# Counting a repeated class of edges: two pairs more per set beside the experts, one set per chunk after them, one set of buffers

## The reference, cut to what matters

```python
h = (x_flat @ W_gat).reshape(M, HEADS, NUM_EXPERTS)
e = leaky_relu(a_src[src] + a_dst[dst], 0.2)      # per edge and head
ee = exp(e - segment_max(e, dst)[dst])
denom = segment_sum(ee, dst)
agg = segment_sum(h[src] * (ee / denom[dst])[:, :, None], dst)
scores = layernorm(agg).mean(heads)
...
for ei in range(4):                               # four experts, every token
    hh = gelu(x @ W1[ei] + b1[ei])
    out += gate[:, ei] * (hh @ W2[ei] + b2[ei])
```

## Time and profile before

| | |
|---|---|
| median of 3 runs | 3698.13 us (3690.57 to 3706.22) |
| the profiled execution's own time | 3702.64 us |
| span of its profile | 3701.0 us |
| mean granted TensorE clock | 0.907 of full speed |
| leading chunks, about 1740 to 2243 us of the span | 503 us |
| late chunks, about 2243 to 2355 us | 112 us |

### The profile page before, as it was taken

How to read it: one execution, slowest core, us unless ns; L and a number is a source line. 1 busy time by engine, 2 the same in 40 slices (tenths; PEclk the granted TensorE clock), 3 DMA queues, 4 the chain that set the end, 5 groups by cost and what they waited for, 6 DMA issues and landing times. The chain is left out here.

```text
span 3701.0 us, 55128 instructions
## 1 busy us (share of the span) xinstructions
PE 2732.4 (74%) x16350; PEld 1679.7 (45%) x16350; DVE 2369.3 (64%) x4532; ACT 1369.6 (37%) x2278; POOL 1087.6 (29%) x1035
## 2 busy tenths in 40 slices
PE   0442123999999999955888785246999999949994
PEld 0332122444444444424665564244655555526662
DVE  9999797787888878776444446794444444433333
ACT  5310100777777878753344341033000000012221
POOL 0000103777773000001655565000111111114442
PEclk9999999999999999975898895557999999969997
DMA  5999895554545445431111111342333333324446
GB/s 194 355 368 410 321 396 192 182 198 176 187 175 196 186 174 201 158 100 29 43 45 42 42 42 16 104 161 81 104 104 103 108 108 103 108 70 124 126 122 195
DMA packets 233854, 568.88 MB, mean 154 GB/s; under 512 B 52113, under 2 KB 93944, under 8 KB 225134
## 3 DMA queue, kind: packets, MB, share of 16 engines
q1 hardware_dynamic: 146006, 376.34, 29.7%
q10 hardware_dynamic: 56152, 163.80, 11.8%
q0 software_dynamic: 31552, 27.13, 3.3%
HBM read 443.12 MB, written 125.87 MB: 154 GB/s over the span
## 5 line engine op out<-in xcount | busy, mean ns | idle before, releaser
L1881 PE MATMUL at_out<-at_pt,top_H 128*128 128x512 f32 x2048 | 931.7, 601 | 34.8 <-ACT at_agg L1733 29.8
L1723 ACT ACTIVATE at_rl<-at_qrow,at_less,at_steep 128x512 f32<-128x512 f32 x1024 | 741.5, 804 | 89.6 <-DVE at_pt L1809 49.6
L1809 DVE SCALAR_TENSOR_TENSOR at_pt<-at_rl,at_turned 128x1024 f32<-128x1024 f32 x512 | 626.2, 1223 | 157.2 <-PE at_out L1881 80.7
L2098 PE MATMUL at_out<-at_parts,at_a 128*128 128x387 bf16 x4096 | 689.3, 328 | 28.8 <-DVE at_parts L2171 15.7
L1881 PEld LDWEIGHTS at_out<-at_pt,top_H 128*128 128x128 f32 x2048 | 373.0, 190 | 439.2 <-issue 396.6
L2098 PEld LDWEIGHTS at_out<-at_parts,at_a 128*128 128x128 fp8e4 x4096 | 399.4, 98 | 305.6 <-issue 36.8
L903 POOL DMA_INDIRECT rec<-at_part x304 | 384.2, 1264 | 104.9 <-issue 93.2
L1161 POOL DMA_INDIRECT edges_GT<-tab,gat_RC x320 | 339.9, 1062 | 237.0 <-DMA edges_GT<-tab,gat_RC 153.0
L2046 POOL DMA_INDIRECT slots<-at_Y,at_dest x128 | 123.2, 962 | 650.7 <-DVEq L2276 614.6
L648 PE MATMUL pack_bp<-top_weights,sort_recs 128*128 128x8 bf16 x1696 | 76.0, 170 | 233.4 <-DMA sort_recs<-in_adj_dram 233.4
L2549 PE MATMUL ex_hp<-ex_XS,ex_WB 128*128 128x512 f32 (+1 forms) x472 | 217.7, 598 | 1.9 <-DMA ex_WB<-wts 1.9
(11 more groups left out here) (551 smaller groups left out, 3695.4 us busy)
## 6 DMA issues: line engine op xcount, KB each, us to landing
sort_recs<-in_adj_dram SPq DMA_DIRECT2D x212, 512.0 KB, 8.9
at_adj<-in_adj_dram SPq DMA_DIRECT2D x192, 512.0 KB
adjT<-at_turned ACTq DMA_DIRECT2D x64, 1024.0 KB
at_a<-adjT SPq DMA_DIRECT2D x128, 512.0 KB
bucket_raw<-in_adj_dram ACTq DMA_DIRECT2D x120, 512.0 KB, 10.2
ex_WB<-wts SPq DMA_DIRECT2D x42, 533.0 KB
y<-f_YB ACTq DMA_DIRECT2D x64, 256.0 KB
f_YB<-y SPq DMA_DIRECT2D x16, 1024.0 KB, 10.4
```

The source lines that it names most:

```text
L1723: ins = nc.scalar.activation(RL[v % NBUF][:, k, :], qrow[:], ACT.Relu, bias=less[:], scale=steep[:, u:u + 1])
L1809: nc.vector.scalar_tensor_tensor(out=PT[v % NBUF][:], in0=RL[v % NBUF][:], scalar=1.0, in1=AT[v // VP % 2][:, 2 * (v % VP):2 * (v % VP) + ...
L1881: ins = nc.tensor.matmul(OUT[:], H[:, u, :], PT[v % NBUF][:, k, :], start=(u == 0), stop=(u == T - 1))
L2098: ins = nc.tensor.matmul(OUT[:, g, x, 0:3 * D1], ones[c % NBUF][:, j, x * P:(x + 1) * P], parts[:, u].rearrange("p k d -> p (k d)"), start ...
```

## The change

Early sets grow from 4 to 6 pairs (3 groups of two pairs), the three late sets of 4 pairs in a late chunk become one set of 4, and there is one set of buffers for all. The pairs counted in this stage go from 17 x 4 + 12 x 4 = 116 to 17 x 6 + 4 x 4 = 118, and `HELD` from 464 to 472. The waits for `late_used` ahead of a late set go.

```diff
-EARLY_SETS, LATE_SETS = 17, 12
-HELD = (EARLY_SETS + LATE_SETS) * 2 * GC
+EARLY_SETS, LATE_SETS = 17, 4
+EARLY_GROUPS, LATE_GROUPS = 3, 2
+HELD = (EARLY_SETS * EARLY_GROUPS + LATE_SETS * LATE_GROUPS) * GC
...
-    PAIRS = 4
+    PAIRS = 2 * EARLY_GROUPS
...
-            OPC = [[spare[1 + s][...] for n in range(PAIRS)] for s in range(2)]
+            OPC = [spare[1 + n // 4][...] for n in range(PAIRS)]
...
-                    def count_hots(s, at, done):
-                        for n in range(PAIRS):
+                    def count_hots(pairs, at, done):
+                        for n in range(pairs):
...
+                    def early_hots(j):
+                        count_hots(2 * EARLY_GROUPS, j * (EARLY_GROUPS * GC), same_hot)
+
+                    def late_hots(i):
+                        count_hots(2 * LATE_GROUPS, (EARLY_SETS * EARLY_GROUPS + i * LATE_GROUPS) * GC, late_hot)
...
-                    def late_hots(g, r):
-                        for i in range(g * IN_LATE, (g + 1) * IN_LATE):
-                            dve.wait_ge(late_used, (off + r) * LATE_SETS + i + 1)
-                            dve.sem_inc(passed, 1)
-                            count_hots((1 + i) % 2, EARLY_SETS + i, late_hot)
...
-                            add_counts(late_used, (off + r) * LATE_SETS + (g + 1) * IN_LATE + 2)
+                            add_counts(late_used, (off + r) * LATE_SETS + g + 1)
...
                     def late_counts(g, r, k):
                         pe.wait_ge(lk_read, k + 2)
                         pe.sem_inc(passed, 1)
-                        for i in range(g * IN_LATE, (g + 1) * IN_LATE):
-                            pe.wait_ge(late_hot, (off + r) * LATE_SETS + i + 1)
-                            pe.sem_inc(passed, 1)
-                            count((1 + i) % 2, range(PAIRS), i % IN_LATE == 0, (i + 1) % IN_LATE == 0).then_inc(late_used, 1)
+                        pe.wait_ge(late_hot, (off + r) * LATE_SETS + g + 1)
+                        pe.sem_inc(passed, 1)
+                        count(range(2 * LATE_GROUPS), 2 * LATE_GROUPS - 1).then_inc(late_used, 1)
...
                                     if e == 2:
                                         early_ready(l * EARLY_SETS + q, k)
-                                        count(g % 2, range(PAIRS // 2), True, False)
+                                        count(range(PAIRS // 2), PAIRS - 1)
                                     output(u + e - 1, e - 1)
                                     if e == 2:
-                                        count(g % 2, range(PAIRS // 2, PAIRS), False, True).then_inc(same_used, 1)
+                                        count(range(PAIRS // 2, PAIRS), PAIRS - 1).then_inc(same_used, 1)
...
                         early_ready(l * EARLY_SETS + EARLY_SETS - 1, (off + LEAD) * RG - 1)
-                        count((EARLY_SETS - 1) % 2, range(PAIRS), True, True).then_inc(same_used, 1)
+                        count(range(PAIRS), PAIRS - 1).then_inc(same_used, 1)
```

More of the change, by code:

```diff
@@ L965, in edge_gates @@
     LEAD = NG // RG
-    PAIRS = 4
-    IN_LATE = LATE_SETS // RG
+    PAIRS = 2 * EARLY_GROUPS
     HK = CK // 2
@@ L971, in edge_gates @@
     assert HID == K * P and K == 2 and NE == 4 and RG == 4 and LEAD == 4
-    assert EARLY_SETS == LEAD * RG + 1 and LATE_SETS == RG * IN_LATE
+    assert EARLY_SETS == LEAD * RG + 1 and LATE_SETS == RG and LATE_GROUPS <= EARLY_GROUPS
     with Phase(nc, "gat") as ph:
@@ L1061, in edge_gates @@
             value = spare[0][:, 4 * HELD:4 * HELD + P * GC].rearrange("p (v c) -> p v c", c=GC)
-            OPC = [[spare[1 + s][:, n * P * GC:(n + 1) * P * GC].rearrange("p (v c) -> p v c", c=GC) for n in range(PAIRS)] for s in range(2)]
-            OFC = [[spare[3][:, (s * PAIRS + n) * T * GC:(s * PAIRS + n + 1) * T * GC].rearrange("p (v c) -> p v c", c=GC)
-                    for n in range(PAIRS)] for s in range(2)]
+            OPC = [spare[1 + n // 4][:, n % 4 * P * GC:(n % 4 + 1) * P * GC].rearrange("p (v c) -> p v c", c=GC) for n in range(PAIRS)]
+            OFC = [spare[3][:, n * T * GC:(n + 1) * T * GC].rearrange("p (v c) -> p v c", c=GC) for n in range(PAIRS)]
             up = pr.sbuf("up", [P, NE, HID])
@@ L1215, in among @@
                         return x.unsqueeze(1).to_broadcast([P, n, x.shape[1]])
-                    def count_hots(s, at, done):
-                        for n in range(PAIRS):
-                            cols = bass.ds(at * (2 * GC) + n // 2 * GC, GC)
-                            ins = one_hots_across(nc, OFC[s][n], OPC[s][n], value, kept[:, 1, n % 2, cols], kept[:, 0, n % 2, cols], T, GC)[1]
+                    def count_hots(pairs, at, done):
+                        for n in range(pairs):
+                            cols = bass.ds(at + n // 2 * GC, GC)
+                            ins = one_hots_across(nc, OFC[n], OPC[n], value, kept[:, 1, n % 2, cols], kept[:, 0, n % 2, cols], T, GC)[1]
                         ins.then_inc(done, 1)
+                    def early_hots(j):
+                        count_hots(2 * EARLY_GROUPS, j * (EARLY_GROUPS * GC), same_hot)
+                    def late_hots(i):
+                        count_hots(2 * LATE_GROUPS, (EARLY_SETS * EARLY_GROUPS + i * LATE_GROUPS) * GC, late_hot)
                     def add_counts(used, number):
@@ L1244, in chunk @@
                         if not leading:
-                            late_hots(g, r)
+                            late_hots(g)
                         dve.wait_ge(gt_in[g], (off + r) * (16 * CK) + 16 * CK)
@@ L1268, in chunk @@
                             add_counts(same_used, l * EARLY_SETS + r * RG + g + 1)
-                            count_hots((g + 1) % 2, r * RG + g + 1, same_hot)
+                            early_hots(r * RG + g + 1)
                         else:
-                            add_counts(late_used, (off + r) * LATE_SETS + (g + 1) * IN_LATE + 2)
+                            add_counts(late_used, (off + r) * LATE_SETS + g + 1)
                     dve.wait_ge(classes_in, 16)
@@ L1294, in _ @@
                         now(nc.vector.tensor_copy(total[:], repeat[:]))
-                        count_hots(0, 0, same_hot)
+                        early_hots(0)
                         assert step.n == AHEAD, step.n
@@ L1450, in scatter, with count @@
                         ins.then_inc(sc_ok, 1)
-                    def count(s, some, opens, closes):
+                    def count(some, last):
                         for n in some:
                             for c in range(GC):
-                                ins = nc.tensor.matmul(HIST, OPC[s][n][:, :, c], OFC[s][n][:, :, c], start=(opens and n == 0 and c == 0),
-                                                       stop=(closes and n == PAIRS - 1 and c == GC - 1), skip_group_check=True)
+                                ins = nc.tensor.matmul(HIST, OPC[n][:, :, c], OFC[n][:, :, c], start=(n == 0 and c == 0),
+                                                       stop=(n == last and c == GC - 1), skip_group_check=True)
                         return ins
@@ L1467, in late_counts @@
                         pe.sem_inc(passed, 1)
-                        for i in range(g * IN_LATE, (g + 1) * IN_LATE):
-                            pe.wait_ge(late_hot, (off + r) * LATE_SETS + i + 1)
-                            pe.sem_inc(passed, 1)
-                            count((1 + i) % 2, range(PAIRS), i % IN_LATE == 0, (i + 1) % IN_LATE == 0).then_inc(late_used, 1)
+                        pe.wait_ge(late_hot, (off + r) * LATE_SETS + g + 1)
+                        pe.sem_inc(passed, 1)
+                        count(range(2 * LATE_GROUPS), 2 * LATE_GROUPS - 1).then_inc(late_used, 1)
                     rounds = rounds_of(pe)
-                    pe.sem_inc(late_used, 2)
                     pe.wait_ge(value_ok, 1)
```

## The result

In 22 runs each the changed kernel takes 3714.15 us (median) against 3701.01 for the kernel before: ratio **1.0033** (95% interval 1.0019 to 1.0046), 13 us slower where 9 us faster was forecast. The profiled execution took 3716.53 us, its span is 3714.9.

What follows compares the result with a forecast made beforehand. TensorE was taken to bound the leading chunks, VectorE the late ones. The terms -35.0 + 22.0 + 3.9 gave -9.1 us, so 3689 us from a median of 3698.13, with a range of 3667 to 3706.

Steps and rivals of the forecast that it cites:

- Late chunks, -35.0: Chunks 16 to 19: dropping two of three one-hot sets shortens VectorE's chain by 35.0 us, with the gather never waited for.
- VectorE's two pairs at nothing: Leading chunks: two more pairs of one-hots, 1.89 us each chunk, are covered by waits and cost nothing.
- Leading matmuls, +22.0: Leading chunks: 16 more counting matmuls each cost TensorE 31.5 us, of which waits cover 9.5, leaving 22.0.
- What stands behind the halves at no cost: Leading chunks: `output` 1 and `hidden` 3, behind the counting halves on TensorE, were given no extra time.
- the clock rival: Leading chunks: halves of 24 counting matmuls let TensorE's clock fall, 58 us in 16 chunks, 3747 us; chance 0.08.
- The set after chunk 15, +3.9: Between leading and late chunks: VectorE's one-hots (1.89) and TensorE's counts (1.97) are in line and add 3.9 us.
- The gather rival: Late chunks: added one-hots delay GpSimd's gathers by 9 to 30 us, so `lg` waits; 3695 us, chance 0.05.
- Hidden counts: Leading chunks: ScalarE's stalls or the gather set their length, so added counts cost nothing; 3667 us, chance 0.18.

Runs made afterwards that it cites:

- e1: The changed kernel with four pairs per leading set on both VectorE and TensorE, pairs 5 and 6 left out of the count; ratio 0.9924.
- e3: The changed kernel with VectorE making six pairs per leading set but TensorE counting only four of them; ratio 0.9899.
- e7: The changed kernel with counts in three parts behind hidden 1, hidden 2 and output 1, and add and next one-hots ahead of the sums; ratio 0.9991.
- f3: The kernel of e8 run again, in one group with the kernel before, f1 and f4; ratio 0.9990.
- e2: The changed kernel with VectorE making four pairs per leading set, TensorE still running 48 counting matmuls, the last 16 on the first two pairs; ratio 1.0030.
- e5: The changed kernel with a leading chunk's 48 counting matmuls in three parts of 16, behind hidden 2, output 1 and hidden 3; ratio 0.9990.
- e9: The changed kernel with all 48 counting matmuls of a leading chunk in one run behind hidden 2; ratio 1.0048.
- e8: The changed kernel with the three parts of e5 and the reordering of e6 together; ratio 0.9944.
- f1: The changed kernel itself, run again in a later group; ratio 1.0028.
- e6: The changed kernel with VectorE, in leading chunks, adding the counts and making the next one-hots ahead of the sums; ratio 0.9972.
- f4: The kernel before with the reordering alone: add of the counts and next one-hots ahead of the sums; 3659.8 us, ratio 0.9957.

## Why the prediction was wrong, point by point

- **Late chunks, -35.0**: right, -35.5. It rests on one thing that I took from the kernel before and that e1, e3, e7 and f3 show to be conditional: that the gather is far ahead.
- **VectorE's two pairs at nothing**: right within some 3 us (e2, e3).
- **Leading matmuls, +22.0**: right; the counts took 23.0 us more in 15 chunks, waits that they cover taken off.
- **What stands behind the halves at no cost: this is the step that failed.** I had `output` 1 and `hidden` 3 keep the higher clock, at 16 counts and at 24, and gave the clock rival 0.08. Its mechanism was right and only its price too high. The fall comes behind one half or the other in ten of 15 chunks and costs 1.0 to 1.7 us each time, 17 us in all, not 3.6 us in every chunk (58). e5, where it comes in none of these chunks, takes 17.8 us less there. Against the kernel before, which loses time in the same place to waits, 6.5 us of it are left in the table. e5 and e9 show that the length of the run makes it: in e5 no fall behind parts of 16, in ten of 15 chunks behind halves of 24, in e9 in all 15 behind 48. (The few falls behind parts of 16 in e8 and f3 have a wait of TensorE of about 1 us or more ahead of them.) My argument against it, that the matmuls of `output` 1 stand between the halves, does not hold: in five chunks `output` 1 is itself what slows down. The Trainium skill, TensorE: Matmul & The Clock Gate, section "HAM oscillation — how this bites in real kernels", puts falls of the clock down to waits of TensorE between groups of matmuls. The trace agrees for `hidden` 1, which stands behind the waits of the look-up (granted clock 0.50 to 0.71 in all 16 chunks). It differs for the falls behind the halves: no wait stands in front of them, only counting matmuls back to back.
- **The wait in front of the look-up, not in the sum**: +8.9 us in the profile (44.4 for 35.5). VectorE's add stands behind the sums and these behind a signal that comes late. In f1 this was 34.9, so this term varies from execution to execution; e6 shows that the order makes it possible.
- **The set after chunk 15, +3.9**: mis-sized, 11.1 measured (8.5 in f1). The two engines' own time is as worked out; a late signal adds 2.6, and what holds the copy back behind the count is not shown.
- Together, on the `adv` of chunk 16: 23.0 for the counts, 6.5 for `output` 1 and `hidden` 3, 8.9 in front of the look-up, 5.1 in the rest of the leading column (`hidden` 1 and `output` 0, behind the look-up's waits, take 7.4 more there) and 11.1 for set 16, less 1.9 ahead of the first scatter: the 52.7 measured for 25.9. So the clock is the step that the prediction looked at and put at nothing, but the look-up (8.9) and set 16 (7.2 over the forecast) miss by as much each. With -35.5 that is +17 at the end of the stage, and 13.9 in the span.
- e5 is 21.9 us longer than before in the leading column, close to the +22.0 of the sum. That is luck: it has 12.0 more in front of the look-up and 11.3 less in `output` 1 and `hidden` 3.
- **The gather rival**: wrong for this kernel. In e1, e3, e7 and f3, whose chunk 16 starts at about 2240 us or earlier, the late chunks do wait for gathers, though not because one-hots slow the gathers down, as the rival had it, but because the chunks come to them sooner. **Hidden counts**: wrong, e2.

What stays open: how GpSimd's gathers hold back TensorE's signals, and why only in the leading chunks. No run here separates the issuing of the DMAs from their traffic.

## What to carry to other kernels

Work moved into a gapless stretch of TensorE is priced with what stands behind it: count how long a run of small matmuls gets, and look in the trace at the clock of the next large ones; split the run where it falls. Before taking a gain at the end of a stage, look at what engine is second there (here the gather) and how far ahead it is once the gain is in. And where an engine works in the order of its program, as VectorE does here, work whose input is there already (the add and the one-hots) goes ahead of a wait for a signal: that alone gained 16 us (f4), where the change lost 13.

## What the runs showed of the hardware that was not expected

- A counting matmul (64 columns) costs 0.12 to 0.13 us at either clock: 24 in 3.06 us at a granted clock of 1.00 (first half of chunk 8), and 64 in 7.95 us at 0.50. It does not suffer from the lower clock, and a long run of them does not keep the higher one (e9).
- Beside the experts, TensorE's signals reach VectorE and ScalarE late (6.4 us in chunk 10 of the changed kernel) while GpSimd issues indirect DMAs in a row, and two can then arrive together; the length of the row sets how late (1.2, 2.5 and 3.7 us in the mean for rows of 2, 4 and 8). In the late chunks the same rows don't do this (0.15 us in the lines above).
- The kernel before took 3700 to 3704 us in the first groups of runs and 3676 in the later ones. Groups of both levels bear the same chip number (5), so it is open what makes the difference: compare within one group.
